# A two-layer graph network on 128 graphs: the product T1 W1 of two graphs as seven products of quarters, and new orders of all queues

## What is computed

```python
# x: (128 graphs, 128 nodes, 512), adj: (128, 128, 128)
# layer 0
h = relu(layernorm(x))
A_hat = A + eye;  d = A_hat.sum(-1) ** -0.5
x = x + (A_hat * d[:, :, None] * d[:, None, :]) @ (h @ W + b)
# layer 1, hypergraph convolution, with H = (adj != 0), w = adj[:, 0, :]
h = relu(layernorm(x))
conv(h, W, b) = Dn * (H @ (Be * (H.T @ (h @ W.T)))) + b
h1 = layer_norm(relu(conv(h, W1, b1)), gamma, beta)   # 512 -> 1024 features
x  = conv(h1, W2, b2) + h + x                         # 1024 -> 512 features
```

## Time and profile before

| | us |
|---|---|
| median of 3 runs (lowest to highest) | 1976.59 (1976.25 to 1977.55) |
| span of the profiled execution | 1974.9 |
| PE busy in it | 1944.6 |
| DVE busy | 1737.6 |
| ACT busy | 1109.5 |
| POOL busy | 1030.2 |

### The profile page before, as it was taken

The page is one execution under the profiler, slowest core; times in us unless marked ns, Lnnn a source line. Parts: engine busy times, 40 slices in busy tenths (PEclk is TensorE's granted clock), DMA queues, the critical chain, the costliest instruction groups (busy, mean ns, idle before and its releaser), DMA issues.

```text
span 1974.9 us, 41437 instructions
## 1 busy us (share of the span) xinstructions
PE 1944.6 (98%) x10310; PEld 935.6 (47%) x10310; DVE 1737.6 (88%) x4388; ACT 1109.5 (56%) x2339; POOL 1030.2 (52%) x1934
## 2 busy tenths in 40 slices
PE   6999999999999999999999999999999999999998
PEld 3444444444444444444444444444444444444443
DVE  7998888888888888888888888888888888888885
ACT  6555555555555555555555555555555555555553
POOL 3545554554555455455545545554554555455544
PEclk9999999999999999999999999999999999999999
DMA  6455444444444444454445444444444544544442
GB/s 188 81 106 102 101 95 103 97 103 96 102 101 95 103 98 103 96 102 100 96 103 97 103 96 101 101 95 103 98 103 96 102 100 96 102 98 103 91 89 63
DMA packets 539836, 197.86 MB, mean 100 GB/s; under 512 B 488016, under 2 KB 504400, under 8 KB 539600
## 3 DMA queue, kind: packets, MB, share of 16 engines
q1 hardware_dynamic: 539600, 195.22, 46.0%
HBM read 48.31 MB, written 33.55 MB: 41 GB/s over the span
## 4 chain that ended last, share of the span: by engine, by line
PE 95%; DVE 2%; issue 1%; DMA 1%; SPq 1%; ACT 1%; POOL 0%; DVEq 0%; POOLq 0%; ACTq 0%
PE ps_u L434 33%; PE ps_c L434 32%; PE ps_e L434 16%; PE ps_c L421 1%; PE ps_c L423 1%; PE ps_c L422 1%; PE ps_e L476 1%; PE ps_y L476 1%; PE ps_e L478 1%; PE ps_e L477 1%; PE ps_y L478 1%; PE ps_y L477 1%; DMA raw_w<-in_W2T_dram 0%; PE ps_p L512 0%; PE ps_p L513 0%
## 5 line engine op out<-in xcount | busy, mean ns | idle before, releaser
L1274 POOL TENSOR_TENSOR dn<-dn,wundo 128x1 f32<-128x1 f32 x128 | 25.1, 196 | 620.0 <-DVE dn L920 619.9
L668 ACT ACTIVATE P_hi<-ps_p 128x128 f16<-128x128 f32 x128 | 35.3, 276 | 490.8 <-PE ps_p L513 490.8
L434 PE MATMUL ps_c<-w1h,t1h 128*128 128x512 f16 x1024 | 262.8, 379 | 2.4 <-ACT t1h L673 2.3
L434 PE MATMUL ps_c<-w1l,t1h 128*128 128x512 f16 x1024 | 262.8, 379 | 0.0
L434 PE MATMUL ps_c<-w1h,t1l 128*128 128x512 f16 x1024 | 262.8, 379 | 0.0
L434 PE MATMUL ps_u<-w2h,hnT_lo 128*128 128x512 f16 x1024 | 241.9, 379 | 0.0
L434 PE MATMUL ps_u<-w2h,hnT_hi 128*128 128x512 f16 x1024 | 241.9, 379 | 0.0
L434 PE MATMUL ps_u<-w2l,hnT_hi 128*128 128x512 f16 x1024 | 241.9, 379 | 0.0
L1263 POOL TENSOR_TENSOR scr<-x1b,xh 128x512 f32<-128x512 f32 x128 | 205.8, 1608 | 20.8 <-POOL base L1198 20.1
L1257 POOL TENSOR_TENSOR x1b<-x,b_all 128x512 f32<-128x512 f32 x128 | 167.7, 1310 | 66.9 <-DVE x L876 65.6
L820 DVE SCALAR_TENSOR_TENSOR z<-ps_c,dn,b_all 128x512 f32<-128x512 f32 x256 | 190.5, 744 | 2.8 <-PE ps_c L434 1.9
(11 more groups left out here) (123 smaller groups left out, 4441.1 us busy)
## 6 DMA issues: line engine op xcount, KB each, us to landing
x_t<-in_x_dram SPq DMA_DIRECT2D x128, 256.0 KB, 2.8
out_dram<-out_t SPq DMA_DIRECT2D x128, 256.0 KB, 2.0
adj_t<-in_adj_dram SPq DMA_DIRECT2D x128, 64.0 KB, 2.5
raw_w<-in_W2T_dram SPq DMA_DIRECT2D x8, 256.0 KB, 6.5
...
A_HT<-A_H SPq DMA_TRANSPOSE x128, 2.4
w_col<-in_adj_dram SPq DMA_DIRECT2D x128, 0.5 KB, 2.5
h0T_hi<-h_hi SPq DMA_TRANSPOSE x128, 2.5
```

What stands on the lines that cost most here:

```text
L434: mm = pe.matmul(ps, t[:, j * 128:(j + 1) * 128], w[:, j, cols], start=(n == 0 and j == 0), stop=(n == 2 and j == blocks - 1))
```

## The change

Graphs are taken in pairs p = (2p, 2p+1). Nearly all per-graph small operations are done once per pair on two columns, A and H of a pair are transposed by one DMA, and `xh_hi`, `xh_lo`, `ahat`, `A_lo`, `P_lo` work on both graphs at once.

T1 W1 of a pair is taken as a 2x2 block product: the rows are the two graphs (256 together), the inner dimension of 512 is cut in two, and the 1024 output features are cut in two. Seven products of blocks replace eight (Strassen's scheme in Winograd's form). `do_M1` to `do_M7` each do one, of 6 matmuls of 512 columns. Four sums of blocks of T1 are needed (S1 to S4, each 128x256 fp32, on POOL), and at the start four sums of blocks of W1. The outputs z are built up by seven DVE instructions (`do_z1` to `do_z7`), where there were four per pair; those of M6, M7 and M4 follow one another in the bank ps_x, and M3 adds to M5 in ps_z.

T1 now goes from PSUM to an fp32 tile `tS` (`do_tf`, ACT), and its parts are made from there: `do_thA` and `do_thS` on ACT, `do_tlA` (768 columns) and `do_tlS` (1024) on DVE. `hn` is made by ACT in place (`do_hn`), no longer by DVE. The small products bias0, nm1 and nm2 move from POOL to DVE. Many tiles get more buffers, some by reuse of the raw weights' space, which is why names such as raw_w and b_all turn up in rows for zh, out_t, y, ul and x1b. All queues have a new order; the steady loop is now one of pairs, k from 7 to 54. At the end of the diff stand the loop of POOL, whole, and the middle of that of DVE.

```diff
-            def do_Y1b(g, i=0):
-                pe.wait_ge(s_t1h, upto(i, g))
-                pe.wait_ge(s_t1l, upto(i, g))
-                wait(pe, s_z[1], i, g - 1)
-                with_weights(Y1[1][:, :], t1h, t1l, w1h, w1l, KI, slice(CH, 2 * CH),
...
+            def quarter(ps, p, t_at, w_at, begins):
...
+                for n, (t, w) in enumerate(((th, w1h), (th, w1l), (tl, w1h))):
+                    for j in range(HK):
+                        mm = pe.matmul(ps[:, :], t[:, t_at - 1, j * 128:(j + 1) * 128], w[:, w_at, j, :],
+                                       start=(begins and n == 0 and j == 0), stop=(n == 2 and j == HK - 1),
...
+            def do_M1(p):
+                pe.wait_ge(s_tha, p + 1)
+                pe.wait_ge(s_tla, p + 1)
+                done(pe, s_z4, p)
+                quarter(ps_x, p, A11, B11, True).then_inc(s_m1, 1)
...
+            def do_M7(p):
+                pe.wait_ge(s_z6, p + 1)
+                quarter(ps_x, p, S3, T3W, False).then_inc(s_m7, 1)
...
-            def do_hn(g, i=0):
-                m = g % 2
-                dve.wait_ge(s_ln2, upto(i, g))
-                dve.tensor_scalar(hn[:, :], h[:, :], sc2[:, m:m + 1], nm2[:, m:m + 1], ALU.mult, ALU.add).then_inc(s_hn, 1)
...
+            def do_tlA(p):
...
+                dve.tensor_tensor(tl[:, 0:3, :], tS[:, A11:A22 + 1, :], th[:, 0:3, :], ALU.subtract).then_inc(s_tla, 1)
...
+            def do_scr2(g):
+                pool.wait_ge(s_xh, g + 1)
+                pool.wait_ge(s_x1b, g + 1)
+                done(pool, s_out, g - 5)
+                pool.tensor_tensor(base[:, g % 6, :], x1b[:, :], xh[:, g % 2, :], ALU.add).then_inc(s_scr2, 1)
...
+            def do_S1(p):
+                pool.wait_ge(s_tf, 2 * p + 2)
+                done(pool, s_tls, p)
+                pool.tensor_tensor(tS[:, S1, :], tS[:, A21, :], tS[:, A22, :], ALU.add).then_inc(s_s1, 1)
...
+            for k in range(STEADY_FROM, STEADY_TO):
+                do_rd0(k+3); do_cx(k+3); do_scr2(2 * k + 2); do_base2(2 * k + 2); do_x1b(2 * k + 3)
+                do_scr2(2 * k + 3); do_base2(2 * k + 3); do_x1b(2 * k + 4); do_dn2(k+2); do_qdn(k+2); do_dn1(k+2)
+                do_S3(k+1); do_S1(k+1); do_S2(k+1); do_S4(k+1); do_u2(k); do_sc2(k); do_u1(k+2); do_sc1(k+2)
...
+            for k in range(STEADY_FROM, STEADY_TO):
+                do_xh_lo(k+1); do_h0_lo(2 * k + 6); do_out(2 * k - 4); do_ul(2 * k - 3); do_z6(k)
+                do_h0_lo(2 * k + 7); do_z2(k); do_out(2 * k - 3); do_hn_lo(2 * k - 1); do_P_lo(k+2)
+                do_x1(2 * k + 4); do_dm(k+2); do_st1(2 * k + 4); do_z5(k); do_ri(k+2); do_aggr1(2 * k + 4); do_z7(k)
+                do_dn(k+2); do_yv(2 * k + 5); do_bn0(2 * k + 8); do_z3(k); do_w_hi(k+5); do_aggr0(2 * k + 8)
...
```

More of the change, by code:

```diff
@@ L129, in bass_adjacency_prenorm_two_layer_gnn_kernel @@
[L129 to L133, removed]
-        base2, out_t = sb("base2", [128, 2, DIN]), sb("out_t", [128, 2, DIN])
-        def bank(name, n=1):
-            return ctx.enter_context(nc.psum_tensor(name, [128, n * CH], F32))
@@ new lines, in do_vq, with do_h0_hi @@
+            def do_vq(g):
+                p, j = g // 2, g % 2
+                act.wait_ge(s_qdn, p + 1)
+                if g == 0:
+                    act.wait_ge(s_v, 1)
+                    act.wait_ge(s_wl[2], KH)
+                done(act, s_base2, g - 1)
+                act.activation(vq[:, j, :], v_all[:, :], ACT.Copy, scale=qdn[:, p % 2, j:j + 1]).then_inc(s_vq, 1)
+            def do_h0_hi(g):
+                p, j = g // 2, g % 2
+                act.wait_ge(s_ln0, p + 1)
+                done(act, s_h0l, g - 1)
+                landed(act, s_tr0h, g - 2)
+                act.activation(h0_hi[:, j, :], x_t[:, g % 4, :], ACT.Relu, bias=bias0[:, p % 2, j:j + 1],
+                               scale=rd0[:, p % 2, j, 0:1]).then_inc(s_h0h, 1)
@@ new lines, in do_h0, with do_yh @@
+            def do_h0(g):
+                p, j = g // 2, g % 2
+                act.wait_ge(s_ln0, p + 1)
+                done(act, s_h0l, g - 1)
+                act.activation(h0[:, j, :], x_t[:, g % 4, :], ACT.Relu, bias=bias0[:, p % 2, j:j + 1],
+                               scale=rd0[:, p % 2, j, 0:1]).then_inc(s_h0, 1)
+            def do_yh(g):
+                j = g % 2
+                act.wait_ge(s_y, g + 1)
+                done(act, s_ay, g - 1)
+                act.activation(yh[:, j, :], y[:, j, :], ACT.Copy, scale=Y_EVAC).then_inc(s_yh, 1)
@@ new lines, in do_hn, with do_hn_hi @@
+            def do_hn(g):
+                p, j = g // 2, g % 2
+                act.wait_ge(s_ln2, p + 1)
+                act.activation(zh[:, g % 4, :], zh[:, g % 4, :], ACT.Identity, bias=nm2[:, p % 2, j:j + 1],
+                               scale=sc2[:, p % 2, j:j + 1]).then_inc(s_hn, 1)
+            def do_hn_hi(g):
+                act.wait_ge(s_hn, g + 1)
+                done(act, s_hnl, g)
+                landed(act, s_trh, g - 1)
+                if g == 0:
+                    act.wait_ge(s_vps, 1)
+                act.activation(hn_hi[:, :], zh[:, g % 4, :], ACT.Copy).then_inc(s_hnh, 1)
@@ new lines, in do_nm2, with do_hn_lo @@
+            def do_nm2(p):
+                m = p % 2
+                dve.wait_ge(s_pp2, p + 1)
+                done(dve, s_hn, 2 * p - 2)
+                dve.scalar_tensor_tensor(out=nm2[:, m, :], in0=st2[:, m, :, 0], scalar=-1.0, in1=sc2[:, m, :],
+                                         op0=ALU.mult, op1=ALU.mult).then_inc(s_ln2, 1)
+            def do_hn_lo(g):
+                dve.wait_ge(s_hnh, g + 1)
+                landed(dve, s_trl, g - 1)
+                if g == 0:
+                    dve.wait_ge(s_vps, 1)
+                dve.tensor_tensor(hn_lo[:, :], zh[:, g % 4, :], hn_hi[:, :], ALU.subtract).then_inc(s_hnl, 1)
@@ L1332, in _, with weight_sums @@
-            weight_power(0)
-            do_rd0(0); do_bias0(0)
+            def weight_sums(n):
+                for j in range(HK if n == 0 else KI):
+                    block_landed(pool, 1, j)
+                done(pool, s_wsums, n)
+                b11, b12 = raw_w1[:, 0:HK, 0:CH], raw_w1[:, 0:HK, CH:DH]
+                b21, b22 = raw_w1[:, HK:KI, 0:CH], raw_w1[:, HK:KI, CH:DH]
+                one, other = ((b12, b11), (b22, raw_t1[:, 0, :, :]), (b22, b12), (b21, raw_t1[:, 1, :, :]))[n]
+                pool.tensor_tensor(raw_t1[:, n, :, :], one, other, ALU.subtract).then_inc(s_wsums, 1)
```

1877 lines of the change are left out of this document (984 added, 893 removed).

## The result

The changed kernel takes 1992.9 us (median of 4 runs, 1991.0 to 1994.7), the kernel before 1976.8 beside it: a ratio of 1.0081 (95% interval 1.0067 to 1.0095). It is slower, where 1956 was forecast; it lies in my range of 1893 to 2012, but on the side to which I gave 0.26.

What follows compares the result with a forecast made beforehand. TensorE was taken to bound the kernel before (PE 98% of span); after the change, waits between DVE, POOL and ACT: 60 x 29.6 + 4 x 28.75 + 51.1 + 12 = 1954 us, plus 1.7, gives 1956; range 1893 to 2012.

Steps and rivals of the forecast that it cites:

- the side to which I gave 0.26: Whole kernel: slower than before, chance 0.26; faster by over 0.2% had 0.67, same 0.07.
- TensorE's gain: TensorE, per pair: 42 matmuls of 512 columns replace 48, saving 1.30 us, to 28.75 us; 64 pairs would save 83 us.
- VectorE's and GpSimd's work: Per pair: DVE gets 0.2 to 0.3 us more, 27.0 in all; POOL's four T1 sums take 0.73 us each.
- The collisions in the loop: DVE instructions with two SBUF inputs and POOL additions block each other: hn_lo loses 1.04 us, dn waits up to 0.7.
- u2 and nm2 behave as described: Loop: POOL's u2 waits for tlA's release (18.3 us), then power sc2 (0.71); DVE's nm2 comes at 19.6.
- The chain's three stretches: Loop round from out(2k-4): 12.2 us to yl, 7.4 to nm2, 9.3 plus 0.6 to out(2k-2), together 29.6.
- The start: Weight loading, W1 splits and sums, and filling by pairs: bounded between nothing and 25 us extra, taken as 12.
- my own sum: Whole span: 60 x 29.6 + 4 x 28.75 + 51.1 + 12 = 1954 us.
- the fill hides behind waits that are there already: Start: pipeline filling by pairs costs nothing extra, as PE idles 16.8 of the first 50 us; the splits don't hide.
- TensorE stays the bound: Rival for the loop: waits from POOL's additions hide; 1893 to 1918 us, put at 1905, PE 97% busy or more; chance 0.25.
- POOL leads: Rival for the loop: T1 sums nearer 1.28 us, or rd0 losing to hn_lo, give a 30.5 us round, 2010; chance 0.21.
- The lock through powers: Rival for the loop: POOL's powers also block DVE's hn_lo and tlS; 31.2 us a round, 2052 us; chance 0.05.

Runs made afterwards that it cites:

- small additions: Changed kernel with GpSimd's three additions (x1b, scr2, base2) on 32 of 512 columns throughout, base zeroed at its start: 1928.3 us, 0.9753 of before.
- The control: Kernel before the change, with its three GpSimd additions on 32 columns for the first 16 graphs and their tiles zeroed: 1975.1 us, ratio 0.9992.
- the kernel without both: Changed kernel with additions on 32 columns for the first 16 graphs, and W1's block sums and their splits on 8 columns: 1952.9 us, 0.9878 of before.
- small additions in the start: Changed kernel with GpSimd's three additions on 32 columns for the first 16 graphs only, base zeroed at its start: 1965.8 us, 0.9943 of before.

## Why the prediction was wrong

**TensorE's gain: right.** 28.75 us a pair was the sum; with small additions the round is 28.80. With four steps moved (hn_lo, x1b, the load of x, aggr2) and the additions whole it is 28.90.

**VectorE's and GpSimd's work: right.** The four sums are at 0.74 to 0.75 us on average in after (I took 0.73). With small additions VectorE is busy 918.9 of 1000 us, 26.5 a round, where I had 27.0.

**The collisions in the loop: right in place and size.** hn_lo lost 0.96 us (forecast 1.04), dn 0.5 (up to 0.7), the gap ahead of the second Y0 is up to 0.78 and 0.44 on average (about 1), u2 and nm2 behave as described. The chain's three stretches, on average over 35 rounds: from out(2k-4) to yl 12.3 us (12.2 in the sum), from yl to nm2 7.0 (7.4), from nm2 to the next out(2k-4) 10.1 (9.9). One link was another: yl does not wait for ScalarE's yh, VectorE's own queue brings it there (I had that queue at 12.0 and yh at 12.2). The round is 29.45 against 29.6; over 60 rounds that is 9 us to the good.

**The start: wrong, and this is the term that turned the sign.** With the measured round my own sum reads 60 x 29.45 + 4 x 28.75 + 51.1 + X = 1989.2, so X is 56 us where I had taken 12 from a range of 0 to 25. The step that failed is "the fill hides behind waits that are there already", and with it that collisions with the additions stood in the sum for the loop and at nothing for the start. I had read those waits on TensorE, 16.8 us in the first 50, and had not asked whose queue would be full: VectorE is busy 190.1 of the 200 us behind them. Three things lie in the 56:
- 27 us are collisions of VectorE with the additions on GpSimd. I had worked these out instruction by instruction for the loop and not at all for the start, where VectorE also makes the parts of W1 and W2 and the layer 0 of the pairs ahead. The control shows that before hardly pays for them (1.5 us).
- 8 us alone, and 13 once the collisions are gone, are the sums of W1 and their splits. I had counted those (three splits of 1.3 us on VectorE, four sums of 2.5 on GpSimd), and my 12 stood for them: for this part it was about right.
- Some 16 us are left (19 if the same sum is made for the profiled execution of the kernel without both, 1950.4 - 60 x 29.42 - 115 - 51.1). They lie in the start as well: in the first 250 us TensorE is busy 208.6 us there and 229.7 in before, with VectorE busy 188 of the last 200. The first T1 of that kernel is 14.4 us later than in before, where x1 of one graph was enough for it. That this lateness is the rest fits the number, but no run took it away, and it stays open.

The first T1 of before, of after, and of the kernel with small additions in the start and no sums of W1 (TensorE):

```profile
39.79 0.22 PE L421 MATMUL ps_c<-P_hi,xh_hi 128*128 128x128 f16 x1 [0.24 <-issue]
```

```profile
64.36 0.26 PE L369 MATMUL ps_t<-P_hi,xh_hi 128*128 128x128 f16 x1 [8.77 <-issue]
```

```profile
54.20 0.27 PE L369 MATMUL ps_t<-P_hi,xh_hi 128*128 128x128 f16 x1 [4.69 <-issue]
```

TensorE's clock is lower in this start. Its instructions behind a wait in after, and the windows before and around them:

```profile
105.57 1.87 PE L381 MATMUL ps_e<-w0h,h0T_hi 128*128 128x512 f16 x4 [2.42 <-DVE x L939]
107.23 1.91 PE L381 MATMUL ps_e<-w0l,h0T_hi 128*128 128x512 f16 x4
```

```profile
91.00:101.00 10.00, 5.54 (x42) 3.13 (x42) 10.00 (x19) 8.14 (x13) 8.83 (x9) 1.00 0.22 52
101.00:111.00 10.00, 6.87 (x16) 2.18 (x17) 10.00 (x19) 4.61 (x13) 5.34 (x8) 0.50 0.38 85
```

1.66 us from one start to the next, where the loop has 0.86: the granted clock is 0.50 (1.2 GHz in place of 2.4) from 101 to 111 us, after 10 us in which TensorE was busy for 5.5. The 0.92 of the window from 50 to 250 us says that about a sixth of those 200 us ran so (0.08 of 0.5). In before the clock is 1.00 there. That this lengthened the kernel is not shown: with small additions in the start it is 0.97, so under half as long at the lower clock, and VectorE, whose queue is the full one, waits no less for it (32.9 us up to tlA(10) against 30.7).

**The rivals.** "TensorE stays the bound" needed four steps moved, and even then the whole is 1967 and not 1905, since the start stays as it is. "POOL leads" came nearer in time (2010, where 1956 was the forecast) by luck, for its mechanism did not happen: no round of 30.5, and the sums at my low end. The lock through powers falls: rd0 ran from 1008.39 to 1009.44 with hn_lo from 1008.75 at its usual 1.23, and from 300 us on all 53 hn_lo and 52 tlS that ran beside a power and no addition took 1.22 us on average, 1.23 at most. The Trainium skill ("SBUF — State Buffer", section "Who interferes with whom") has the pair of ports held for a whole instruction; the traces agree for additions and not for powers. The same section also says that a `tensor_scalar` can take the shared pair, where its operands allow it, and that I should have used: HB_hi and A_H, which have one SBUF input that is a tensor, go from 254 and 275 ns to 580 and 647 beside additions, while I had priced instructions with two such inputs alone.
